# Two-step graph network with nucleus attention: the second step's first tile gathered during the rank stage, and the first step's references copied before the last self additions

## The chip, the cores and the metric

The kernel runs on one core of a Trainium2 chip. TensorE (PE) does the matrix products, VectorE (DVE) the sorting, masking and searching, ScalarE (ACT) the exponentials, GpSimd (POOL) small sums and the indirect transfers, and SyncE (SP) issues the large transfers. The metric is the device time of one launch in microseconds, lower is better. Before the change it is 1792.87 us, the median of three runs (1787.85 to 1796.46).

## The reference

N is 4096 nodes, D is 128 features, the attention projections have 64 columns. R is the adjacency matrix plus the identity, divided by its row sums. Cut to what matters:

```
def _top_p_attention(X, W1, W2, W3):
    q = X @ W1.T @ W2.T
    k = X @ W3.T
    probs = softmax(q @ k.T)
    idx = argsort(-probs); sp = probs sorted; cs = cumsum(sp)
    keep_sorted = cs - sp < 0.9          # the smallest set that holds 0.9
    A = probs * mask
    return A / max(A.sum(-1), 1e-12)

R = S + eye(N); R = R / R.sum(-1)
Z = 0; Xf = X; Xa = X
for n in range(2):
    A = _top_p_attention(Xa, W1, W2, W3)
    Xf = R @ Xf
    Xa = A @ Xa
    Z = Z + Xf @ U1[n].T + Xa @ U2[n].T
h = X + Z
... layer norm of h with gain and shift, then a layer norm of x + that
```

## The kernel before, in words

Both steps of the network run the same three stages. The 4096 rows are cut in 8 blocks of 512, each block in 4 tiles of 128 rows.

**Rank stage** (`rank_block`). For each block PE forms the logits of 512 rows against all 4096 columns, DVE takes the 8 largest of each chunk (MAX8) and sorts out the largest 24 (step 1) or 64 (step 2) of each row (`sort_step`), ACT sums the exponentials. From these DVE computes where the nucleus ends (`stats_step`). This is done for a block while the next one is under way; for the last block it stands by itself at the end of the stage, after 16 sort steps for its last tile. A row whose nucleus doesn't fit the sorted numbers is called hard. Its number goes into `list_dram`, block by block: POOL issues 4 indirect transfers for each block once DVE has placed its rows. Beside it PE multiplies with the adjacency matrix (`adj_part`), whose 64 parts of 1 MB SP loads into a ring of 4 buffers (`adj_in`); each load waits until PE has used the buffer's last content. Before a part that holds the diagonal is used, POOL adds the identity to it (`add_self`).

**Tiles of hard rows.** When all of the list is written, POOL fetches 128 of its entries (`gid`, `gids`), then by indirect transfers the rows' features, references (`href`, `hrefs`) and largest exponentials (`htop`, `htops`). PE transposes the tile, forms its q and its 16 logit products, ACT exponentiates, and DVE searches each row's threshold (`halve`, `chord`, then two passes, MAX8 and sorting). Where a row isn't settled by the sorted 40 numbers, a branch of 24 more sums over the whole row is run (`tile_settle`, `dve.If`). The resulting cuts and norms go to `cut_dram` and `norm_dram` by two indirect transfers.

- In step 1 there is one tile. In program order POOL does: 4 fetches of `gather(0)`, `add_self` of block 6, `add_self` of block 7, then in the loop the copies `gid_out`, `htop_out`, `href_out`, and then `gather(1)`. The next tile's fetch is always made, even where there is none. DVE's search reads the copies. DVE takes the low half of the next tile's q (L1676, `prepare(c + 1)`) at the end of its search. PE and ACT meanwhile finish the adjacency product of blocks 6 and 7.
- In step 2 there are four. The first is gathered, transposed, exponentiated and searched by itself between the rank stage and the loop over the blocks, the others are searched within that loop. Ahead of the first tile stand the last block's z terms (`z_terms` on PE, `other_copy` on ACT, `add_x` on POOL, `z_rows` on DVE), each in two halves.

**Mix stage.** For each block PE forms the transposed logits with the cuts subtracted, ACT exponentiates, DVE masks, PE weighs. In step 1 the adjacency's rows are summed beside it; in step 2 the layer norms are.

The order of the work is written out by hand on each engine. An engine goes through its instructions in order, and a wait holds up all that stands behind it. SP's loads are one queue: in step 1 (L434 to L437) `flow_load` runs through all 64 parts, with the stores of the cuts (`rank_store`) between them, and in step 2 (L441) the stores of block i - 2 come after the 8 loads of block i.

Of the kernel before, what the change touches and what calls it, by code (L numbers as in the profile page):

```python
# [6 lines left out]
FP32 = mybir.dt.float32  # L7
# [8 lines left out]
def gnn_kernel(  # L16
# [71 lines left out]
    LIST = N + (PAIRS - 1) * P  # L88
    LAG1 = 3
# [5 lines left out]
    with ctx:  # L95
# [189 lines left out]
        def step_sems(s):  # L285
# [10 lines left out]
            if s == 0:  # L296
                names += ["h_l", "h_exp", "h_done", "m_l_ps", "m_exp_done"]
                names += ["r_n_ps", "r_n_sb", "m_n_ps", "m_y_sb", "m_yt_ps", "m_yt_sb", "xa_out"]
                names += ["sum_act", "sum_dve", "xf_scaled"]
            else:  # L300
                names += ["slot_full", "slot_read", "h_read"]
                names += ["r_z_ps", "r_zo_sb", "r_zx_sb", "r_z_sb", "m_z_ps", "m_z_add", "var_sb", "rstd_sb", "centred", "normed", "res_sb"]
# [88 lines left out]
        def _(sp):  # L391
# [8 lines left out]
            for s in range(STEPS):  # L400
                g = S[s]

                def rank_loads(i, first):

                    for r in range(PARTS):
                        if not (first and r < RING):
# [5 lines left out]

                def rank_store(i):

                    sp.wait_ge(g["st_cut"], i + 1)
                    rows = bass.ds(i * TB, TB)
                    with nc.allow_non_contiguous_dma(reason="cuts go out in row order"):
                        sp.dma_start(cut_dram[s][bass.ds(i * BI, BI), :].rearrange("(t p) o -> p (t o)", p=P),
                                     ncut[:, rows]).then_inc(g["cut_out"], 16)
                        if s > 0:  # L420
                            sp.dma_start(ref_dram.rearrange("(p t) o -> p (t o)", p=P)[:, rows],
                                         ncut[:, rows]).then_inc(g["cut_out"], 16)
                        for dst, src in ((norm_dram, norm), (top_dram, top_exp)):
                            sp.dma_start(dst[s].rearrange("(p t) o -> p (t o)", p=P)[:, rows],
                                         src[:, rows]).then_inc(g["cut_out"], 16)
# [7 lines left out]
                if s == 0:  # L433
                    for n in range(NB * PARTS):  # L434
                        flow_load(n)
                        if n >= 12 and n % FLOWS == 0 and (n - 12) // FLOWS < NB:
                            rank_store((n - 12) // FLOWS)  # L437
                else:
                    rank_loads(0, True)
                    rank_loads(1, False)  # L440
                    with sp.Fori(2, NB) as i:  # L441
                        rank_loads(i, False)
                        rank_store(i - 2)
# [72 lines left out]
        def _(pool):  # L516
# [32 lines left out]
            for s in range(STEPS):  # L549
# [21 lines left out]
                assert JQ == TB and PARTS == NB  # L571
                SELF_BEFORE = {0: (0, 1), 1: (2,), 2: (3,), 4: (4,), 5: (5,)}
                if s > 0:
                    add_self(0)
                for i in range(NB):
                    if s == 0:
                        for a in SELF_BEFORE.get(i, ()):
                            add_self(a)
                    else:
                        if i < RING - 1:  # L580
                            add_self(i + 1)
                        add_x(i, 0)
                        if RING - 1 <= i < NB - 1:
                            add_self(i + 1)
                        add_x(i, 1)
                    pool.wait_ge(g["st_place"], i + 1)
                    for t in range(i * TB, (i + 1) * TB):
# [4 lines left out]
                            bounds_check=N - 1, oob_is_err=False).then_inc(g["listed"], 16)  # L592
                pool.wait_ge(g["listed"], 16 * T)
                if s > 0:
                    pool.wait_ge(S[s - 1]["xa_out"], 16 * NB)
                pool.wait_ge(g["counted"], 1)

                if s == 0:
# [15 lines left out]
                    gather(0)  # L614
                    for a in range(FLOWS, NB):
                        add_self(a)
                    with pool.Fori(0, tiles) as c:
                        pool.wait_ge(g["h_x"], c * 48 + 48)
# [4 lines left out]
                        pool.wait_ge(g["h_ref"], c + 1)  # L623
# [14 lines left out]
                        pool.wait_ge(g["h_out"], c * 32 + 32)  # L638
                    pool.sem_inc(g["h_done"], 1)
                else:  # L640
                    sweeps = pool.value_load(count[0:1, 0:1], min_val=1, max_val=SWEEPS)

                    def gather_tile(r, c):

                        st = tile_slot(c)
                        if c >= 2:
                            pool.wait_ge(g["h_out"], r * (PT * 32) + (c if c == PT + 1 else c - 1) * 32)
                        pool.dma_start(gids[:, st, :], list_dram[s][bass.ds(r * (PT * P) + c * P, P), :]).then_inc(g["h_gid"], 16)
                        pool.wait_ge(g["h_gid"], r * (PT * 16) + (c + 1) * 16)
                        pool.sem_inc(met, 1)  # L650
                        nc.gpsimd.indirect_dma_start(
                            out=xgs[:, st, :], out_offset=None, in_=source,
                            in_offset=bass.IndirectOffsetOnAxis(ap=gids[:, st, 0:1], axis=0),
                            bounds_check=N - 1, oob_is_err=False).then_inc(g["h_x"], 16)
                        pool.wait_ge(g["cut_out"], 64 * NB)
                        for dst, src in ((hrefs, ref_dram), (htops, top_dram[s])):
                            nc.gpsimd.indirect_dma_start(
                                out=dst[:, st:st + 1], out_offset=None, in_=src,
                                in_offset=bass.IndirectOffsetOnAxis(ap=gids[:, st, 1:2], axis=0),
                                bounds_check=N - 1, oob_is_err=False).then_inc(g["h_ref"], 16)  # L660
# [43 lines left out]
                    gather_tile(0, 0)  # L704
# [18 lines left out]
        def _(pe):  # L723
# [5 lines left out]
            for s in range(STEPS):  # L729
# [122 lines left out]

                def ranks(i):
# [10 lines left out]
                if s == 0:  # L864
                    pe.wait_ge(g["r_o_sb"], FLOWS)
                    for j in range(0, JT // 4):
                        adj_part(FLOWS, j)
                ranks(NB - 1)
                pe.wait_ge(g["st_tally"], NB)
                if s == 0:  # L870
                    to_rows(FLOWS - 1)
                    for j in range(JT // 4, FLOWS * JQ):
                        adj_part(FLOWS, j)
# [7 lines left out]
                if s == 0:  # L881
# [25 lines left out]
                    for j in range(FLOWS * JQ, JT):  # L907
# [71 lines left out]
                else:  # L979
                    sweeps = pe.value_load(count[0:1, 0:1], min_val=1, max_val=SWEEPS)  # L980

                    def tile_rows(r, c):

                        pe.wait_ge(g["h_x"], r * (PT * 16) + (c + 1) * 16)
                        nc.tensor.transpose(psT[:, 0, :], xgs[:, tile_slot(c), :], ident[:]).then_inc(g["h_xt"], 1)

                    def tile_q(r, c):

                        pe.wait_ge(g["h_xts"], r * PT + c + 1)
                        nc.tensor.matmul(psQ[:, 0:P], wq[:], xgT[:], start=True, stop=True).then_inc(g["h_q"], 1)  # L990

                    def tile_logits(r, c, n, bank):

                        if n == 0:
                            pe.wait_ge(g["h_qlo"], r * PT + c + 1)
# [1219 lines left out]
```

## Time and profile before

| | us |
|---|---|
| median of three runs | 1792.87 |
| the profiled execution | 1791.29 |
| its span, first to last instruction | 1789.7 |
| PE busy in the span | 1536.5 (86%) |
| DVE busy | 1335.8 (75%) |
| ACT busy | 785.9 (44%) |
| POOL busy | 231.0 (13%) |

The mean granted clock of PE is 0.934 of full speed. The page also cuts the span in 40 slices of 44.7 us and gives the busy share of each engine in tenths; in the first step the rank stage lasts to about 337 us, the mix stage starts at about 466; in the second they are about 1227 and 1321. In the timeline a row is: start, duration, engine, line, operation, output<-input, number of instructions, and in brackets the idle time of the engine before it and what ended it. "issue" there is a wait whose releaser the profile doesn't show.

### The profile page before, as it was taken

The page shows a single profiled execution, that of the slowest core. Times are in us where ns is not written, and L with a number is a line of the kernel's source. Part 1 is how long each engine was busy: PE and PEld are TensorE (multiplying, and loading weights), DVE is VectorE, ACT ScalarE, POOL GpSimd, SP SyncE. Part 2 cuts the span into 40 slices and gives each one's busy share as a digit, 9 for nine tenths or more (in the row PEclk, how much of TensorE's full clock was granted, in tenths as well). Part 3 has the DMA queues.
Part 4 walks back from the last instruction along what each step waited for, and adds up shares of the span by engine and source line. Part 5 has one row for each costly group of instructions (what it writes and reads, how often), then busy time and mean ns, then how long its engine had stood idle before and what let it go on. Part 6 is the DMA issues. An engine that isn't in the chain of part 4 may idle for free. (4 is left out here: it accounts for less than half of the span.)

```text
span 1789.7 us, 18143 instructions
## 1 busy us (share of the span) xinstructions
PE 1536.5 (86%) x4753; PEld 885.9 (50%) x4753; DVE 1335.8 (75%) x3740; ACT 785.9 (44%) x1245; POOL 231.0 (13%) x264
## 2 busy tenths in 40 slices
PE   6999999772799999998999999992247878888995
PEld 3556555331455555554555656562124535544553
DVE  4788888408477777776899999994868888897553
ACT  3555555210455555555444444441223424434443
POOL 1010211113000000000011111112010121211322
PEclk9999999976799999999999999995668999999997
DMA  7457665740255555555556666630000000000000
GB/s 241 171 142 147 193 202 165 179 169 6 95 188 193 193 193 193 193 194 206 202 172 185 184 175 185 186 118 2 2 2 1 1 7 6 4 4 7 7 7 12
DMA packets 52364, 211.88 MB, mean 118 GB/s; under 512 B 21760, under 2 KB 30528, under 8 KB 31664
## 3 DMA queue, kind: packets, MB, share of 16 engines
q1 hardware_dynamic: 49008, 210.56, 37.1%
q0 software_dynamic: 3264, 0.30, 0.2%
q8 instruction: 33, 0.54, 0.1%
q14 instruction: 59, 0.48, 0.1%
HBM read 206.63 MB, written 4.45 MB: 118 GB/s over the span
## 5 line engine op out<-in xcount | busy, mean ns | idle before, releaser
L1607 DVE MAX8 cand<-psL 128x8 f32<-128x256 f32 (+1 forms) x640 | 371.1, 581 | 58.9 <-PE psL L818 51.9
L1175 ACT ACTIVATE psL<-psL,umax 128x1024 f32<-128x1024 f32 x256 | 278.5, 1088 | 295.0 <-DVE umax L1601 294.6
L817 PE MATMUL psL<-kA,mq 128*128 128x512 f32 x512 | 299.6, 585 | 7.7 <-DVE mq L1434 7.7
L788 PE MATMUL psO<-adj_in,xn 128*128 128x512 f32 x512 | 242.5, 595 | 3.6 <-DMA adj_in<-in_adjT 1.8
L964 PE MATMUL psO<-ebuf,xn 128*128 128x512 f32 x512 | 241.4, 593 | 0.0
L788 PE MATMUL psO<-adj_in,xf 128*128 128x512 f32 x512 | 240.9, 595 | 0.0
L1868 DVE SCALAR_TENSOR_TENSOR ebuf<-ebuf 128x1024 f32<-128x1024 f32 x128 | 156.7, 1224 | 99.7 <-PE psO L964 93.2
L1313 ACT ACTIVATE ebuf<-psL 128x1024 f32<-128x1024 f32 x128 | 129.8, 1021 | 191.3 <-PE psL L1022 134.7
L818 PE MATMUL psL<-kB,mq 66*128 66x512 f32 x512 | 203.4, 397 | 0.0
L1250 ACT ACTIVATE ebuf<-psL 128x1024 f32<-128x1024 f32 x128 | 131.0, 1023 | 133.8 <-PE psL L936 133.8
L1034 PE MATMUL psO<-xf,xa 128*128 128x512 f32 x340 | 167.6, 616 | 19.0 <-DVE xf L2075 19.0
L1021 PE MATMUL psL<-mq,kA 128*128 128x512 f32 x256 | 151.2, 591 | 10.9 <-DVEq L2068 10.9
L935 PE MATMUL psL<-mq,kA 128*128 (+1 forms) x256 | 148.2, 579 | 3.2 <-DVEq L1835 3.2
L2075 DVE SCALAR_TENSOR_TENSOR xf<-ebuf 128x1024 f32<-128x1024 f32 x85 | 105.9, 1250 | 48.5 <-PE psO L1034 30.2
L817 PEld LDWEIGHTS psL<-kA,mq 128*128 128x128 f32 x512 | 97.3, 190 | 79.0 <-issue 53.9
L788 PEld LDWEIGHTS psO<-adj_in,xn 128*128 128x128 f32 x512 | 95.7, 190 | 77.7 <-issue 64.4
L964 PEld LDWEIGHTS psO<-ebuf,xn 128*128 128x128 f32 x512 | 96.7, 190 | 74.9 <-issue 63.9
L788 PEld LDWEIGHTS psO<-adj_in,xf 128*128 128x128 f32 x512 | 95.8, 190 | 74.6 <-issue 66.0
L818 PEld LDWEIGHTS psL<-kB,mq 66*128 66x128 f32 x512 | 97.7, 191 | 69.6 <-issue 57.8
L561 POOL TENSOR_TENSOR adj_in<-adj_in,ident 128x128 f32<-128x128 f32 x64 | 28.0, 467 | 696.3 <-DMA adj_in<-in_adjT 696.3
L1921 DVE SCALAR_TENSOR_TENSOR xf<-adj_in,htry 128x2048 f32<-128x2048 f32 x48 | 112.6, 2346 | 0.4
L1022 PE MATMUL psL<-mq,kB 66*128 66x512 f32 x256 | 104.4, 408 | 0.0
(353 smaller groups left out, 2050.9 us busy)
## 6 DMA issues: line engine op xcount, KB each, us to landing
adj_in<-in_adjT SPq DMA_DIRECT2D x128, 1024.0 KB, 5.5
adj_in<-in_adj SPq DMA_DIRECT2D x32, 2048.0 KB, 7.6
xaT<-in_xT SPq DMA_DIRECT2D x1, 2048.0 KB, 7.8
xa_dram<-xa SPq DMA_DIRECT2D x8, 256.0 KB, 7.8
out<-t SPq DMA_DIRECT2D x8, 256.0 KB, 2.3
list_dram<-ids,place POOLq DMA_INDIRECT x64, 4.4
rel_prob<-cut_dram SPq DMA_DIRECT2D x32, 2.0 KB
cut_dram<-ncut SPq DMA_DIRECT2D x16, 2.0 KB
```

Source lines behind the costliest of these rows:

```text
L788: last = nc.tensor.matmul(psO[:], fs[:, j, :], adj_in[:, r % RING, j % JQ, :], start=(j == 0), stop=(j == JT - 1))
L817: nc.tensor.matmul(o, qA[:, t * P:(t + 1) * P], kA[:, c:c + BI], start=True, stop=False)
L818: last = nc.tensor.matmul(o, qB[0:DA + 2, t * P:(t + 1) * P], kB[0:DA + 2, c:c + BI], start=False, stop=True)
L935: nc.tensor.matmul(o, kA[:, j * P:(j + 1) * P], mqA(i), start=True, stop=False)
L964: last = nc.tensor.matmul(psO[:], xs[:, j, :], ekept[:, u % 2, hb * BI:(hb + 1) * BI], start=(j == 0), stop=(j == JT - 1))
L1021: nc.tensor.matmul(o, kA[:, j * P:(j + 1) * P], mqA(i), start=True, stop=False)
L1034: last = nc.tensor.matmul(psO[:], xs[:, j, :], kept_unit(n)[:, hb * BI:(hb + 1) * BI], start=(j == 0), stop=(j == JT - 1))
L1175: nc.scalar.activation(ps[:], ps[:], ACT.Exp, bias=umax[:, bass.ds(i * UB + k, 1)], scale=1.0, accum_out=usum[:, bass.ds(i * UB + k, 1)]). ...
L1250: nc.scalar.activation(eraw[:, u % 2, :], psL[buffer(u, MU)][:], ACT.Exp).then_inc(g["m_exp_done"], 1)
L1313: nc.scalar.activation(raw_unit(n), psL[w % 3][:], ACT.Exp).then_inc(g["slot_read"], 1)
L1607: last = v.max(cand[:, t % 2, at + c * 8:at + c * 8 + 8], psL[(turn + k) % 3][:, c * WIDE:(c + 1) * WIDE])
L1868: v.scalar_tensor_tensor(out=ekept[:, u % 2, :], in0=eraw[:, u % 2, :], scalar=1.0, in1=eraw[:, u % 2, :], op0=ALU.is_ge, op1=ALU.mult).th ...
```

## The change

It has three parts. First, in step 1 the three copies are made right after `gather(0)`, before the two `add_self`; the loop copies the next tile's at its end. Second, in step 1 SP issues only 52 of the 64 loads, then the last `rank_store`, then waits until the three fetches of `gather(0)` have landed, and only then issues the last 12; PE does 8 parts' worth of products fewer (j from 16 to 24) before that tile and 8 more after it. Third, in step 2 the first tile's list is fetched after six blocks (`EARLY` is 6), its rows in block 7; PE, ACT and DVE do its q, logits and exponentials around the last block's sorting; the last block's z terms come after the logits, with `z_rows` inside the search; and the position in the list is raised to at least 128 after the sixth block. The stores of the cuts of block i - 2 are moved between the first and second load of block i. Those of the last two blocks signal a semaphore of their own (`cut_late`), and the two tables are filled with ones in step 1.

```
@@ step 1, SP
-                    for n in range(NB * PARTS):
+                    held = FLOWS * PARTS + RING
+                    for n in range(held):
                         flow_load(n)
-                        if n >= 12 and n % FLOWS == 0 and (n - 12) // FLOWS < NB:
+                        if n >= 12 and n % FLOWS == 0:
                             rank_store((n - 12) // FLOWS)
+                    rank_store(NB - 1)
+                    sp.wait_ge(g["h_x"], 48)
+                    for n in range(held, NB * PARTS):
+                        flow_load(n)
+                    for dst in (ref_dram, top_dram[1]):
+                        sp.dma_start(dst..., ones[:, 0:T]).then_inc(S[1]["cut_late"], 16)
@@ step 2, SP
+                        if r == 1 and ended is not None:
+                            rank_store(ended)
@@ step 2, POOL (add_self, add_x and list_rows as before, but for the order)
+                    for i in range(NB - 1):
+                        if i < RING - 1:
+                            add_self(i + 1)
+                        add_x(i, 0)
+                        if i == EARLY:
+                            tile_fetch(0, 0)
+                        if i >= RING - 1:
+                            add_self(i + 1)
+                        add_x(i, 1)
+                        list_rows(i)
+                        if i == EARLY - 1:
+                            pool.wait_ge(g["listed"], 16 * EARLY * TB)
+                            tile_list(0, 0)
+                    list_rows(NB - 1)
+                    add_x(NB - 1, 0)
+                    add_x(NB - 1, 1)
@@ step 1, POOL
+                    gather(0)
+                    kept_copies(0)
+                    for a in range(FLOWS, NB):
+                        add_self(a)
+                    with pool.Fori(0, tiles) as c:
...
                         pool.wait_ge(g["h_out"], c * 32 + 32)
+                        kept_copies(c + 1)
                     pool.sem_inc(g["h_done"], 1)
@@ after the rank stage, PE
                 if s == 0:
                     pe.wait_ge(g["r_o_sb"], FLOWS)
-                    for j in range(0, JT // 4):
+                    for j in range(0, RING * JQ // 2):
                         adj_part(FLOWS, j)
+                else:
+                    tile_rows(0, 0)
+                    tile_q(0, 0)
+                    pe.wait_ge(g["r_exp_done"], NB * UB)
+                    for n in range(NU):
+                        if n >= 3:
+                            pe.wait_ge(g["slot_read"], n - 2)
+                        tile_logits(0, 0, n, n % 3)
                 ranks(NB - 1)
@@ step 2, DVE
+                    if s > 0 and n == SORTS - 4:
+                        tile_q_lo(0, 0)
                     sort_step(TB - 1, n)
...
                     tile_begin(0, 0, NU)
                     for n in range(19):
                         search_step(0, 0, n)
-                        if n == 3:
+                        if n == 2:
+                            z_rows(NB - 1, 0)
+                        if n == 5:
+                            z_rows(NB - 1, 1)
+                        if n == 12:
                             tile_q_lo(0, 1)
```

On POOL, from the first fetch of step 1's tile on, the order before is this (`gid` is the list's entries, `xg` the features, L561 the identity's addition for two blocks, L617 the loop's start):

```order
L603 DMA gid<-list_dram0 128x2
L609 DMA xg<-in_x,gid 128x128
L609 DMA href<-cut_dram0,gid 128x1
L609 DMA htop<-top_dram0,gid 128x1
L561 TENSOR_TENSOR adj_in<-adj_in,ident 128x128 x8
L617 UNCONDITIONAL_BRANCH
L617 ISA
L620 COPY gid_out<-gid 128x2
L621 COPY htop_out<-htop 128x1
L622 COPY href_out<-href 128x1
```

and in the changed kernel, same place:

```order
L658 DMA gid<-list_dram0 128x2
L664 DMA xg<-in_x,gid 128x128
L664 DMA href<-cut_dram0,gid 128x1
L664 DMA htop<-top_dram0,gid 128x1
L673 COPY gid_out<-gid 128x2
L674 COPY htop_out<-htop 128x1
L675 COPY href_out<-href 128x1
L573 TENSOR_TENSOR adj_in<-adj_in,ident 128x128 x8
L682 UNCONDITIONAL_BRANCH
```

The three copies have moved ahead of the 8 additions.

On ACT, from the last exponential of the rank stage of step 2 to the second tile, before (L1175 the rank stage's exponentials, L1159 and L1160 those of the last block's statistics, L1137 the z terms' copies, L1281 and L1286 a tile's transpose and q, L1294 its exponentials):

```order
L1175 ACTIVATE psL,usum<-psL,umax 128x1024
L1159 ACTIVATE ue<-ud 128x16
L1160 ACTIVATE rel_prob<-rel_prob 128x256
L1164 ACTIVATE top_exp<-top_rel 128x4
L1165 ACTIVATE ehalf<-half 128x4
L1137 COPY t<-psT 128x256 x2
L1276 TENSOR_LOAD count
L1276 ISA x2
L1281 COPY xgT<-psT 128x128
L1286 CAST hq<-psT 128x128
L1294 ACTIVATE adj_in,hsum<-psL,hrefs 128x1024 x4
```

and in the changed kernel:

```order
L1217 ACTIVATE psL,usum<-psL,umax 128x1024
L1239 COPY xgT<-psT 128x128
L1244 CAST hq<-psT 128x128
L1252 ACTIVATE adj_in,hsum<-psL,hrefs 128x1024 x2
L1201 ACTIVATE ue<-ud 128x16
L1202 ACTIVATE rel_prob<-rel_prob 128x256
L1252 ACTIVATE adj_in,hsum<-psL,hrefs 128x1024 x2
L1206 ACTIVATE top_exp<-top_rel 128x4
L1207 ACTIVATE ehalf<-half 128x4
L1179 COPY t<-psT 128x256 x2
```

The tile's work has moved ahead of the last block's statistics, with two of its four exponentials in front of the pair that DVE's statistics wait for.

On SP, the last loads of step 1, before (L431 a load, L418 and L424 the stores of a block, L458 the read of the norms at the start of the mix stage):

```order
L431 DMA adj_in<-in_adjT 128x2048 x6
L418 DMA cut_dram0<-ncut 128x4x1
L424 DMA norm_dram0<-norm 128x4
L424 DMA top_dram0<-top_exp 128x4
L431 DMA adj_in<-in_adjT 128x2048 x9
```

and in the changed kernel:

```order
L435 DMA adj_in<-in_adjT 128x2048 x3
L410 DMA cut_dram0<-ncut 128x4x1
L416 DMA norm_dram0<-norm 128x4
L416 DMA top_dram0<-top_exp 128x4
L435 DMA adj_in<-in_adjT 128x2048 x12
L448 DMA ref_dram<-ones 128x32
```

Three loads have moved behind the last block's stores, and the wait for the tile stands in front of the 12.

## Rows read from the trace of the kernel before

**Rows 1.** The page's slices: PE's busy tenths, 44.7 us each.
```profile
PE   6999999772799999998999999992247878888995
```

**Rows 2.** Timeline of DVE, the tile of step 1.
```profile
370.17 0.28 DVE L1676 TENSOR_TENSOR mq<-psT,mq 64x128 fp32r<-64x128 f32 x1 [31.17 <-ACT mq L1218]
378.86 0.16 DVE L1756 TENSOR_REDUCE htotal<-hsum 128x1 f32 x1 [8.40 <-ACT xa L1226]
...
406.48 0.15 DVE L1760 TENSOR_SCALAR hupper<-htop_out 128x1 f32<-128x1 f32 x1 [27.21 <-POOL href_out L622]
...
407.44 4.49 DVE L1702 SCALAR_TENSOR_TENSOR ebuf<-xa,htry 128x4096 f32<-128x4096 f32 x1
...
436.24 4.48 DVE L1688 SCALAR_TENSOR_TENSOR ebuf<-xa,htry 128x4096 f32<-128x4096 f32 x1
...
452.47 0.28 DVE L1676 TENSOR_TENSOR mq<-psT,mq 64x128 fp32r<-64x128 f32 x1
```

**Rows 3.** Timeline of POOL, the tile of step 1.
```profile
356.92 0.60 POOL L603 DMA_DIRECT2D gid<-list_dram  x1 [12.88 <-issue]
363.08 1.07 POOL L609 DMA_INDIRECT xg<-in_x,gid  x1 [5.56 <-DMA gid<-list_dram]
...
404.13 1.69 POOL L561 TENSOR_TENSOR adj_in<-adj_in,ident 128x128 f32<-128x128 f32 x4 [35.68 <-DMA adj_in<-in_adjT]
...
406.26 0.18 POOL L622 COPY href_out<-href 128x1 f32<-128x1 f32 x1
...
410.16 2.68 POOL L609 DMA_INDIRECT xg<-in_x,gid  x1 [2.25 <-DMA gid<-list_dram]
...
418.34 4.92 POOL L609 DMA_INDIRECT htop<-top_dram,gid  x1 [0.30 <-issue]
```

**Rows 4.** Timeline of PE, the same stretch.
```profile
332.78 3.70 PE L788 MATMUL psO<-adj_in,xn 128*128 128x512 f32 x8 [1.82 <-DMA adj_in<-in_adjT]
...
368.24 0.45 PE L887 MATMUL psT<-ident,xg 128*128 128x128 f32 x1 [16.71 <-DMA htop<-top_dram,gid]
...
377.13 7.03 PE L788 MATMUL psO<-adj_in,xn 128*128 128x512 f32 x16
...
385.40 27.63 PE L788 MATMUL psO<-adj_in,xn 128*128 128x512 f32 x64
...
424.44 0.48 PE L887 MATMUL psT<-ident,xg 128*128 128x128 f32 x1 [10.01 <-DMA htop<-top_dram,gid]
```

**Rows 5.** Stretch; busy of PE, PEld, DVE, ACT, POOL; clock; DMA share; GB/s.
```profile
330.00:345.00 15.00, 12.86 (x37) 5.97 (x36) 5.38 (x29) 0.89 (x3) 3.89 (x4) 1.00 0.99 390
```

**Rows 6.** Timeline of POOL, the fetch of step 2's first tile.
```profile
1241.80 0.58 POOL L648 DMA_DIRECT2D gids<-list_dram  x1 [2.30 <-issue]
1244.95 1.05 POOL L651 DMA_INDIRECT xgs<-xa_dram,gids  x1 [2.57 <-DMA gids<-list_dram]
```

**Rows 7.** Timeline of DVE, end of step 2's rank stage and first search.
```profile
1214.89 0.29 DVE L1578 MAX8 top<-cand 128x8 f32<-128x128 f32 x1
...
1217.00 0.17 DVE L1472 SCALAR_TENSOR_TENSOR ue<-usum,ue 128x16 f32<-128x16 f32 x1 [0.65 <-ACT rel_prob L1160]
...
1227.36 0.15 DVE L1667 TENSOR_SCALAR count<-s 128x1 int32<-128x1 f32 x1
...
1229.56 0.61 DVE L1524 SCALAR_TENSOR_TENSOR z<-psT,rinv,t 128x128 f32<-128x128 f32 x2 [1.04 <-POOL t L569]
...
1249.62 0.28 DVE L1901 TENSOR_TENSOR hq<-psT,hq 64x128 fp32r<-64x128 f32 x1 [14.46 <-ACT hq L1286]
1257.32 0.16 DVE L1907 TENSOR_REDUCE htotal<-hsum 128x1 f32<-128x4 f32 x1 [7.42 <-ACT adj_in L1294]
...
1307.38 0.16 DVE L2021 TENSOR_TENSOR hkept<-hkept,habove 128x1 f32<-128x1 f32 x1
```

**Rows 8.** Timeline of ACT, the tile's first exponential.
```profile
1252.14 1.11 ACT L1294 ACTIVATE adj_in<-psL,hrefs 128x1024 f32<-128x1024 f32 x1 [2.54 <-PE psL L1000]
```

**Rows 9.** The page's costliest groups: the half-row sums of step 2's searches.
```profile
L1921 DVE SCALAR_TENSOR_TENSOR xf<-adj_in,htry 128x2048 f32<-128x2048 f32 x48 | 112.6, 2346 | 0.4
```

More of the change, by code:

```diff
@@ L401, in _, with rank_store, rank_loads @@
                 g = S[s]
-                def rank_loads(i, first):
+                def rank_store(i):
+                    sp.wait_ge(g["st_cut"], i + 1)
+                    rows = bass.ds(i * TB, TB)
+                    over = g["cut_late"] if s > 0 and i >= EARLY else g["cut_out"]
+                    with nc.allow_non_contiguous_dma(reason="cuts go out in row order"):
+                        sp.dma_start(cut_dram[s][bass.ds(i * BI, BI), :].rearrange("(t p) o -> p (t o)", p=P),
+                                     ncut[:, rows]).then_inc(over, 16)
+                        if s > 0:
+                            sp.dma_start(ref_dram.rearrange("(p t) o -> p (t o)", p=P)[:, rows],
+                                         ncut[:, rows]).then_inc(over, 16)
+                        for dst, src in ((norm_dram, norm), (top_dram, top_exp)):
+                            sp.dma_start(dst[s].rearrange("(p t) o -> p (t o)", p=P)[:, rows],
+                                         src[:, rows]).then_inc(over, 16)
+                def rank_loads(i, first, ended):
                     for r in range(PARTS):
+                        if r == 1 and ended is not None:
+                            rank_store(ended)
                         if not (first and r < RING):
@@ L411, in rank_loads @@
                         sp.dma_start(adj_in[:, r % RING], adjT[i, :, r * JQ:(r + 1) * JQ, :]).then_inc(g["adj_in"][r % RING], 16)
[L413 to L425, printed above, removed]
                 def flow_load(n):
@@ L569, in add_x, with gather_tile @@
                     nc.gpsimd.tensor_tensor(t2[:, 0:ZT, :], t2[:, 0:ZT, :], xn[:, rows, :], ALU.add).then_inc(g["r_zx_sb"], 1)
[L571 to L578, printed above, removed]
-                    else:
[L580 to L585, printed above, removed]
+                def gather_tile(r, c):
+                    if c >= 2:
+                        pool.wait_ge(g["h_out"], r * (PT * 32) + (c if c == PT + 1 else c - 1) * 32)
+                    tile_list(r, c)
+                    tile_fetch(r, c)
@@ L612, in gather, with kept_copies @@
                                 bounds_check=N - 1, oob_is_err=False).then_inc(g["h_x"], 16)
[L614 to L618, printed above, removed]
+                    def kept_copies(n):
+                        pool.wait_ge(g["h_x"], n * 48 + 48)
                         pool.sem_inc(met, 1)
@@ L871, in _ @@
                     to_rows(FLOWS - 1)
-                    for j in range(JT // 4, FLOWS * JQ):
+                    for j in range(RING * JQ // 2, RING * JQ):
                         adj_part(FLOWS, j)
@@ L906, in _ @@
                     prepare_logits(0)
-                    for j in range(FLOWS * JQ, JT):
+                    for j in range(RING * JQ, JT):
                         adj_part(FLOWS, j)
```

161 lines of the change are left out of this document (87 added, 74 removed).

## The prediction

> **What bounds the kernel now.** I read the page's slices first. PE is full nearly throughout and falls to 2 tenths in slice 10 and to 2, 2 and 4 in slices 28 to 30 [rows 1]. These are the two places where a step goes from ranking to mixing, and the change lies in both. So I read the timelines there, engine by engine, and asked who waits for whom.
>
> In step 1 DVE has the tile's sum at 378.86 and goes on at 406.48, 27.21 us later; the releaser is POOL's copy of the references [rows 2]. POOL had long had the data: it stood at block 7's identity, for a load that came at 404.13, and copied after it [rows 3]. Then DVE searches without a break until 452.47, the low half of the next q [rows 2]. PE needs 27.63 us for block 7 beside that wait, until 413.03, and is then waiting itself for the next tile's fetch until 424.44 [rows 4]. The end of this stage is therefore POOL's copy plus DVE's search, 46 us. Before it there is a second wait: POOL issued the last list transfer by 344.04 and could go on only at 356.92, then the list's own fetch took until 363.08 [rows 3]. The same two waits in step 2 are 2.30 us, and 3.15 from 1241.80 to 1244.95 [rows 6]. What differs is the traffic: in 330 to 345 us the queues are 0.99 busy at 390 GB/s [rows 5], and PE itself waits there for a part [rows 4]. So in step 1 the small transfers stand behind 1 MB loads.
>
> In step 2 DVE ends the last block's statistics at 1227.36. The first tile's search begins at 1257.32, and in the 30 us between DVE works little over 2 [rows 7]. POOL does the z terms, then the list, then the tile. The search goes to 1307.5, with DVE alone busy. Only then can the mixing begin.
>
> **Step 1: the held loads.** After load 51 nothing large is queued until the tile has landed. Part 49 landed at 332.78 [rows 4]; at 1 MB in 2.7 us (390 GB/s, rows 5) parts 50 and 51 are in by 338.2, before the last block's list transfers, which end at 344.04. So I take step 2's waits: 344.04 + 2.30 + 3.15 = 349.49 for the first indirect fetch. From there to PE's transpose it was 368.24 - 363.08 = 5.16 [rows 3, 4], so the tile lands at 354.65 and not at 368.24: 13.6 us earlier. The bounds: nothing, if the wait isn't the traffic, and 13.6. I take the upper one, as the rows of step 2 are the same instructions with idle queues. PE loses the cover: 8 parts' products less before the tile (7.03 us per 8 [rows 4]) are done after it, and the first held load must land before PE ends the logits (8.9 us after the tile). Four loads from a standing start take perhaps 2.3 us and then 2.7 each, so the first has some 4 us to spare.
>
> **Step 1: the copies.** They come at 355.3 now, and DVE isn't held. Its sum comes at 378.86 - 13.6 = 365.3, the search goes on about 0.4 later, and 46.0 us on (452.47 - 406.48) it is at L1676, at 411.7. What is late next is that instruction's other input, the next tile's q. PE ends block 7 at 377.13 - 13.6 + 35.9 (to 413.03) + 6.9 (8 parts) = 406.3. POOL adds block 7's identity as before 8.9 us earlier, at 397.4. There DVE is in its last long pass (436.24 to 440.7, moved by 41, is 395.5 to 399.9). POOL's work beside such passes takes long: the indirect fetches of 1.07 and 1.05 [rows 3, 6] took 2.68 and 4.92 there [rows 3]. So I let the additions wait for the end of the pass and take 1.7 from 400: 401.7. From there 3.7 to the indirect fetch (406.44 to 410.16) and 5.2 to PE, at 410.6, and 1.9 to q (368.24 to 370.17 [rows 2, 4]): 412.5. It decides by 0.8 us. The stage is 452.5 - 412.5 = 40.0 shorter. Against it stand the three copies at the loop's end, in front of the signal for the norms, 0.6 us (405.82 to 406.44 [rows 3]). Step 1: **39.4 us**. Below, if the held loads bring nothing, only the 27.2 of the wait go, less 0.6: 26.6, as the next q would be there at about the same time as the search's end (424.44 + 1.9). Above, no wait for q: 40.2.
>
> The two fills with ones lie behind the last load on SP, which then waits anyway.
>
> **Step 2: the tile ahead.** The list is fetched in block 6's time and the rows in block 7's, some 30 us before PE is free for them, and the tile is filled from the same list. The moved stores hold SP's second load of a block by about one unit of the 16 of a block, and that load is needed 5 units later; I count nothing, and some us if that cover is gone. DVE takes q's low half 4 sort steps before the last, at about 1213.8 (the steps, 0.36 each, end with that of 1214.89 [rows 7]). In the trace a first exponential starts 2.5 us after that instruction (1249.62 to 1252.14), and one is 1.11 and its read 0.2 [rows 7, 8]. So the two in front of the statistics' exponentials end at about 1213.8 + 2.5 + 2.6 = 1218.9, or 1.5 earlier with PE at full clock. These statistics ended at 1217.0 for DVE [rows 7], the pair takes 0.5: DVE goes on at 1219.4, 2.4 later, between 1 and 3. The other two lie in DVE's statistics. The statistics then end at 1229.8, one memset follows, and the search's first instruction is at 1230.6 in place of 1257.32: **26.7 us** earlier. Inside the search now are the two `z_rows`, 0.61 each [rows 7]: 1.2. Their sums on POOL stand behind the list's last 4 transfers, which begin at 1228.9 and run partly beside the passes of 2.35 us [rows 9]. By the row with 4.92 each such instruction may wait for the end of one pass: 2 transfers and `add_x` so come to about 1238, and DVE wants them after three passes, at 1240. I take no wait; above it is 3. The second tile's fetch, about 12 us under the same passes, is through by 1260, and its q is wanted after 12 search steps, near 1270; its exponentials need 8 us, DVE's rest 12. It stays covered. Step 2: 26.7 - 1.2 = **25.5 us**, between 22 and 27.
>
> **The sum.** 39.4 + 25.5 = 64.9. The profiled execution is 1791.29, 1.6 below the median of the runs shown. 1791.3 - 64.9 = 1726.4. All that follows either place moves with it, as the mixing starts only from its cuts.
>
> **The Trainium skill** bears on POOL beside DVE. Its page "SBUF — State Buffer", section "SBUF: two separate sides", says that DVE and GpSimd share a port pair as an exclusive lock for a whole instruction, where a DVE operation with two SBUF inputs meets a GpSimd one, and that whoever comes first blocks the other. The trace agrees for POOL (4.92 beside DVE's 4.49 us passes). For DVE no pass here is longer for it: 4.49 and 4.48. By the page DVE would also start late after each POOL instruction; in step 2 that would be some five starts by up to 1 us, and the sum 1731 instead of 1726.
>
> **The rivals.**
> *The loads aren't what held the list* (12 in 100). Against it rows 5 and 6, for it that the 12.88 has no named releaser. Then step 1 gives 26.6: 1791.3 - 26.6 - 25.5 = 1739.
> *POOL loses beside DVE's passes what it gained* (18 in 100). The identity of block 6 waits for the third held load, about 10 us after the tile; DVE's first long pass begins 11.7 after it (406.48 to 407.44 after a sum that comes 10.6 after the tile). If the load is 2 us later, four additions go between passes of 4.49, and PE gets the part 6 to 10 us late; the gathering for the next q goes with it, so step 1 gives 30 to 35. With 2 or 3 us of waiting for `add_x` in step 2 that is 1791.3 - 32.5 - 23 = 1736.
> *Slower: the search's branch is taken* (3 in 100). The first tile now reads references and largest values while the last two blocks are not yet written. If a single row of a tile got a wrong one, `dve.If` runs 24 sums in two halves of 2.35 us with half a us between, 24 x 4.7 + 12 = 125 us: 1726 + 125 = 1851. The point is one flagged row. In before there are 48 such halves in all, 12 for each of four tiles [rows 9], so no row is flagged, and the first tile's rows are from blocks that are stored; if they weren't full, the page's groups would show more than 48.
> *The change doesn't do what it says in step 1* (3 in 100): the search isn't what ends the stage, because the next tile's fetch can't come before block 7's identity and that comes as late as before. Then only step 2's 25.5 remain: 1766.
>
> **How the numbers follow.** The forecast has 62 in 100, its own range 1721 to 1732. The rivals have 12, 18, 3 and 3, and 2 are left for what I don't see. The range of 8 in 10 is 1716 to 1744: down by what PE at full clock would save at either start of mixing and by the spread of the runs shown, up to both likely rivals and the median's 1.6. About 0.5% (9 us) is what a measurement of this kernel can tell from no change. All but the branch lie far beyond it: faster 0.95, within 0.02, slower 0.03.
>
> **What would show it.** In the changed profile: POOL's first list fetch at about 346 and PE's transpose at 355; no wait of DVE for `href_out`; L1676's counterpart at about 412; the mixing of step 1 starting near 427 instead of 466. In step 2 the search's first sum about 1 us after the count instead of 30, and 48 half-row sums. Wrong would be a long wait of PE for POOL's identity in block 6, of DVE for POOL at `z_rows`, or a fetch of the list that still takes 13 us.

## The result, and the profile after

| | before | after |
|---|---|---|
| median (lowest to highest), us | 1791.10 (1787.85 to 1796.46), 4 runs | 1723.93 (1723.05 to 1725.26), 4 runs |
| the profiled execution, us | 1791.29 | 1724.79 |
| its span; mean granted clock of PE | 1789.7; 0.934 | 1723.2; 0.947 |
| mixing begins in step 1, in step 2 (first matmul, us) | 466.29, 1321.08 | 426.47, 1255.83 |

The ratio is 0.9623, interval 0.9596 to 0.9649: 67 us faster, 5 either way. The forecast was 1726.4.

The page of the changed kernel, PE's slices, against [rows 1]:

```profile
PE   6999999977999999998999999994267979888995
```

Slice 10 has 7 instead of 2. The hole at 28 to 30 is 4, 2, 6 instead of 2, 2, 4.

The timeline of POOL in step 1 (start, duration, engine, line, operation, output<-input, count, idle time before and its releaser), against [rows 3]:

```profile
344.21 0.97 POOL L619 DMA_INDIRECT list_dram<-ids,place  x1 [0.30 <-issue]
348.28 0.60 POOL L658 DMA_DIRECT2D gid<-list_dram  x1 [3.10 <-issue]
351.18 1.07 POOL L664 DMA_INDIRECT xg<-in_x,gid  x1 [2.30 <-DMA gid<-list_dram]
...
356.87 0.18 POOL L675 COPY href_out<-href 128x1 f32<-128x1 f32 x1
366.02 1.69 POOL L573 TENSOR_TENSOR adj_in<-adj_in,ident 128x128 f32<-128x128 f32 x4 [8.96 <-DMA adj_in<-in_adjT]
398.52 4.31 POOL L573 TENSOR_TENSOR adj_in<-adj_in,ident 128x128 f32<-128x128 f32 x4 [30.82 <-DMA adj_in<-in_adjT]
```

The list is fetched 3.10 us after its last transfer instead of 12.88, its own fetch takes 2.30 instead of 5.56, and the copies are done before the identity of block 6. PE in the same stretch, against [rows 4]:

```profile
356.33 0.45 PE L956 MATMUL psT<-ident,xg 128*128 128x128 f32 x1 [10.52 <-DMA htop<-top_dram,gid]
...
379.74 27.63 PE L828 MATMUL psO<-adj_in,xn 128*128 128x512 f32 x64
...
410.49 0.33 PE L956 MATMUL psT<-ident,xg 128*128 128x128 f32 x1 [1.72 <-DMA htop<-top_dram,gid]
...
426.47 0.50 PE L1004 MATMUL psL<-mq,kA 128*128 128x512 f32 x1 [3.33 <-DVEq L1895]
```

The next tile's rows are waited for 1.72 us instead of 10.01. DVE, against [rows 2]:

```profile
366.81 0.14 DVE L1820 TENSOR_SCALAR hupper<-htop_out 128x1 f32<-128x1 f32 x1
...
368.00 4.48 DVE L1762 SCALAR_TENSOR_TENSOR ebuf<-xa,htry 128x4096 f32<-128x4096 f32 x1
...
413.02 0.28 DVE L1736 TENSOR_TENSOR mq<-psT,mq 64x128 fp32r<-64x128 f32 x1
```

There is no wait for `href_out`, and none for the next q. In step 2 DVE shows this, against [rows 7]:

```profile
1179.09 0.18 DVE L1521 SCALAR_TENSOR_TENSOR ue<-usum,ue 128x16 f32<-128x16 f32 x1 [3.10 <-ACT rel_prob L1202]
...
1189.46 0.15 DVE L1727 TENSOR_SCALAR count<-s 128x1 int32<-128x1 f32 x1
...
1190.54 0.16 DVE L1962 TENSOR_REDUCE htotal<-hsum 128x1 f32<-128x4 f32 x1 [0.17 <-DVEq L1444]
...
1242.61 0.16 DVE L2076 TENSOR_TENSOR hkept<-hkept,habove 128x1 f32<-128x1 f32 x1
```

The search begins 1.1 us after the count instead of 30. It lasts 52.1 us, 2.0 more than before. The half-row sums are 48 again, against [rows 9] (count, then busy and mean ns, then idle):

```profile
L1976 DVE SCALAR_TENSOR_TENSOR xf<-adj_in,htry 128x2048 f32<-128x2048 f32 x48 | 112.9, 2353 | 0.3
```

The mixing of step 1 begins 39.8 us earlier, that of step 2 65.25, so step 2 gave 25.4. The span is 66.5 shorter; the last 1.3 us lie behind the start of step 2's mixing and aren't explained.

### The profile page after: what moved, and what is told of

The parts are those of the page before. It is cut to its first block and busy times, and to the rows that moved or that the text cites. A ratio compares the mean times of both kernels' runs of the same rounds, so it can differ in the third digit from the quotient of the medians.

```text
span 1723.2 us, 17953 instructions
## 1 busy us (share of the span) xinstructions
PE 1536.2 (89%) x4753; PEld 886.1 (51%) x4753; DVE 1338.1 (78%) x3740; ACT 786.3 (46%) x1245; POOL 232.6 (13%) x267
## 3 DMA queue, kind: packets, MB, share of 16 engines
HBM read 206.63 MB, written 4.48 MB: 123 GB/s over the span
## 5 line engine op out<-in xcount | busy, mean ns | idle before, releaser
L1069 PE MATMUL psL<-mq,kA 128*128 128x512 f32 x256 | 151.2, 591 | 10.4 <-DVEq L2123 10.4
```

Of the source, the lines that this page charges most:

```text
L1069: nc.tensor.matmul(o, kA[:, j * P:(j + 1) * P], mqA(i), start=True, stop=False)
```

## The experiments

Three comparisons were made, each on one chip with the kernel before beside it. That kernel's median was 1797.44, 1800.93 and 1794.89 there. The second and third also had the changed kernel as control: 1733.69 (ratio 0.9627, interval 0.9614 to 0.9641) and 1727.01 (0.9622, 0.9608 to 0.9636). For the two control runs this was expected:

> The changed kernel itself, as control for the others of this call: 0.9623 of before, within 0.0026.

> The changed kernel, control of this call: 0.9623 to 0.9627 of before.

A ratio is good to 2 or 3 us at best, and the difference of two to about 4 (6 in the first comparison, which is set against the ratio of the result above). So I also read from each trace how long it is from the last list transfer of step 1 to the first matmul of the mixing. In the changed kernel that is 344.21 to 426.47, 82.3 us (81.8 and 81.5 in the controls); before it was 343.07 to 466.29, 123.2.

### Is it the hold? Loads not held

```
- held = FLOWS * PARTS + RING ... sp.wait_ge(g["h_x"], 48)
+ for n in range(NB * PARTS): flow_load(n), stores at n = 12, 18, ... 54
- PE: parts 0 to 3 of block 6 ahead of the tile
+ PE: parts 0 to 5
```

A part here is a load of 1 MB, of which PE makes 8 products. The "8 parts' worth" in the description of the change are 8 calls of `adj_part` with 2 products each (the 7.03 us are x16 in the timeline), so they are two of these 1 MB parts.

> The changed kernel, but step 1's 64 loads go out as their slots come free, as before, and PE does block 6's parts as early as before; the copies stay ahead. Theory (the small list transfers stand behind 1 MB loads): POOL's first list fetch comes some 13 us after the last list transfer again instead of 3.1, PE's transpose of the tile at 368 instead of 356.3, the search and the start of mixing some 12 us later: 1724 + 12 = 1736 (1734 to 1739). Rival (the wait has another cause, and the loads were held for nothing): the fetch at 348, 1722 to 1726.

Measured: 1743.58, ratio 0.9698 (0.9679 to 0.9718), 13 us above the changed kernel's ratio, 6 either way. From the last list transfer to the mixing it is 98.1 us, 15.9 more. POOL:

```profile
364.58 0.60 POOL L653 DMA_DIRECT2D gid<-list_dram  x1 [15.28 <-issue]
370.41 1.07 POOL L659 DMA_INDIRECT xg<-in_x,gid  x1 [5.24 <-DMA gid<-list_dram]
...
411.51 9.71 POOL L568 TENSOR_TENSOR adj_in<-adj_in,ident 128x128 f32<-128x128 f32 x4 [33.45 <-DMA adj_in<-in_adjT]
```

Both waits are back, 12.2 and 2.9 longer, and the rival (the fetch at 348, no time lost) is out. Block 7's identity also falls among DVE's long passes and takes 9.71 instead of 1.69 to 4.3. All of this edit, which also puts the stores back behind the loads, is worth the forecast's 13.6, or a little more.

### How much traffic does it take? The hold alone undone on SP

The same, but PE keeps its 4 parts, so only 4 loads can go out.

> The changed kernel, but SP does not wait for the tile before load 52; PE still does only 4 parts of block 6 ahead of the tile. So four more loads of 1 MB go out, one as each of the 4 parts is used, from about 334 to 345, and the rest after the tile. Theory (the queue must be empty, in proportion to what is in it): those four need 11 us, so the queues are busy until about 347 to 350 and the list fetch comes 3 to 6 us later than in the changed kernel: 1727 to 1731. Rival (any load under way costs all of it): 1736. Rival (only the long queue of before costs): 1724.

Measured: 1737.95, ratio 0.967 (0.965 to 0.969), about 8 us more than the changed kernel; 91.9 us to the mixing, 9.7 more. POOL:

```profile
361.56 0.60 POOL L653 DMA_DIRECT2D gid<-list_dram  x1 [12.96 <-issue]
```

With four loads the wait for the list is about what it was with the long queue of the kernel before (12.88); my 3 to 6 us were too few. By the list's wait this is the first rival, that any load under way costs all of it (its time, 8 more and 6 either way, can't tell the two apart). But by the loads alone it is odd: the last of the four goes out at 349.26, one takes 2.7 us by [rows 5], and POOL waits until 361.56. The queues in that stretch (busy of PE, PEld, DVE, ACT, POOL; clock; DMA share; GB/s):

```profile
350.00:355.00 5.00, 0.00 (x0) 0.00 (x0) 0.00 (x0) 0.00 (x0) 0.00 (x0) 0.79 1.09 57
```

They are full with 57 GB/s, where the 1 MB loads moved 390 [rows 5]. Of the 848 packets of these 5 us 814 are under 512 bytes; nearly all of the bytes are in the 34 others, the rest of a load. SP's rows show whose the small ones are. First the changed kernel:

```profile
335.79 0.40 SPq L410 DMA_DIRECT2D cut_dram<-ncut  x1
```

Then this one:

```profile
322.33 23.82 SPq L435 DMA_DIRECT2D adj_in<-in_adjT  x6
346.20 0.43 SPq L410 DMA_DIRECT2D cut_dram<-ncut  x1
```

The last block's three stores (2 KB each, in packets under 512 bytes) stand on SP behind loads that wait for their slot. They go out 10.4 us later, of which 3.4 are the rank stage's. In the changed kernel they stand 8.4 us ahead of the last list transfer, here 1.4, beside the four. So it was in the kernel before, whose list transfers ran from 339.24 to 343.07:

```profile
341.63 0.43 SPq L418 DMA_DIRECT2D cut_dram<-ncut  x1
```

### Loads or stores? Each alone

```
loads not held, stores ahead:      - sp.wait_ge(g["h_x"], 48)
loads held, stores beside the list: + sp.wait_ge(g["st_place"], NB)
                                      rank_store(NB - 1)
```

> The changed kernel, but SP does not wait for the tile before load 52; the last block's three stores stay ahead of that load, as in the changed kernel. So it differs from the run with loads not held (SP only) in the place of the three stores alone. There the list fetch came 13.0 us after the last list transfer, and after the 1 MB loads the queues were busy for 7 us more with packets under 512 bytes at some 40 GB/s. Theory L (1 MB loads under way hold the list): the list fetch is 10 us or more after the last list transfer, 0.967 of before as there. Theory S (the stores' small packets, queued behind the loads and beside the list, hold it): it comes after 3 to 5 us, at most 6, and the time is within 3 us of the changed kernel, 0.962 to 0.964.

> The changed kernel with all its held loads, but SP gives out the last block's three stores only when the last places are known, so that they run beside the four list transfers with no 1 MB load under way. Theory S (the stores' small packets hold the list): the list fetch comes 6 to 10 us after the last list transfer instead of 3.1, the time is 3 to 6 us longer. Theory L: the fetch comes after 3 to 4 us; the references' fetch may wait a little for the stores; within 1.5 us of the changed kernel.

Measured: 1740.39 and 1737.12 against the control's 1733.69, that is 6.7 and 3.4 us more (ratios 0.9657, 0.9642 to 0.9673, and 0.9645, 0.963 to 0.9659; by these 5.4 and 3.2 more, 4 either way, so the second isn't clear of the noise by its time). From the last list transfer to the mixing it is 87.6 and 87.0 us instead of 81.8. POOL, first with the loads not held and the stores ahead:

```profile
352.57 0.97 POOL L618 DMA_INDIRECT list_dram<-ids,place  x1 [0.30 <-issue]
360.67 0.60 POOL L657 DMA_DIRECT2D gid<-list_dram  x1 [7.13 <-issue]
```

Then with the loads held and the stores beside the list, and the queues in that stretch and in the last 6 us of POOL's wait, in the columns of above:

```profile
347.25 0.39 SPq L410 DMA_DIRECT2D cut_dram<-ncut  x1
...
351.85 0.97 POOL L620 DMA_INDIRECT list_dram<-ids,place  x1 [0.30 <-issue]
360.90 0.60 POOL L659 DMA_DIRECT2D gid<-list_dram  x1 [8.08 <-issue]
```

```profile
347.00:361.00 14.00, 6.43 (x15) 2.50 (x14) 0.53 (x4) 0.19 (x1) 3.99 (x5) 0.90 0.04 1
354.00:360.00 6.00, 0.00 (x0) 0.00 (x0) 0.00 (x0) 0.00 (x0) 0.00 (x0) 0.84 0.00 0
```

The control:

```profile
354.69 0.60 POOL L658 DMA_DIRECT2D gid<-list_dram  x1 [2.64 <-issue]
```

Neither theory holds alone. The control waits 2.64 us for the list. Loads alone make it 7.13, stores alone 8.08, both 12.96: 4.5 and 5.4 add up to 9.9, and 10.3 was measured (9.9 against the 3.10 of the first changed profile). The stores do it with the queues 4% busy, and from 354 to 360, while POOL waits, nothing at all moves on them. So it isn't their bytes. Nor is it the program: POOL's fetch of the list waits for the list transfers' semaphore and for the count, and only the fetch of the references behind it waits for the stores'. Why the signal of the list's end comes so late the profile doesn't show.

### Is it the copies?

```
  gather(0)
- kept_copies(0)
  for a in range(FLOWS, NB): add_self(a)
  loop over tiles:
+     kept_copies(c)
```

> The changed kernel, but the three copies stand behind both additions of the identity again, as before; the loads stay held. Theory (DVE's search waits for href_out, and POOL gives it after block 7's identity, whose part now comes at 398 to 402): DVE has the sum at 366.8 and goes on at about 403.5, 36.7 us later; the mixing starts 36 us later: 1724 + 36 = 1760 (1757 to 1763). That would leave to the held loads alone 3 us against the kernel with neither. Rival (terms simply add, 27 for the copies): 1751.

Measured: 1761.51, ratio 0.98 (0.9778 to 0.9822), 32 us more, 6 either way; 116.1 us to the mixing, 33.9 more. The time alone doesn't tell my 36 from the rival's 27, the trace does. DVE:

```profile
402.14 0.15 DVE L1819 TENSOR_SCALAR hupper<-htop_out 128x1 f32<-128x1 f32 x1 [33.95 <-POOL href_out L675]
```

The wait is the price, to a tenth. It is 2.8 less than I expected: with DVE waiting, block 7's identity takes 1.69 and not 4.31. So the parts of the change are no sum. With the copies late the hold is worth 7.4 us (123.5 in the next run less 116.1), with the copies ahead 15.9.

### Step 2 alone

The hold and the copies are both undone, step 2 is as changed.

> Step 1 as before (loads not held, PE's parts as before, copies late), step 2 as changed. Theory (the two places add up): step 1's 39.4 come back: 1724 + 39.4 = 1763 (1761 to 1767), 0.984 to 0.986 of before. Rival (one part's gain needs the other): under 1757 or over 1770.

Measured: 1770.07, ratio 0.9845 (0.9825 to 0.9866), 40 us more, 6 either way; 123.5 us to the mixing, as before (123.2). The two places add up. Within step 2 only the order of two exponentials and the place of the stores were varied (below); what the early fetch, the early logits and the moved `z_rows` give each wasn't measured.

### The two exponentials in front

```
  tile_rows_copy(0, 0); tile_q_hi(0, 0)
- for n in range(2): tile_exp(...)
  stats_prob(NB - 1)
+ for n in range(NU): tile_exp(...)
```

> The changed kernel, but on ACT in step 2 the last block's two exponentials for the probabilities come before all four of the tile's, not after two of them. Theory (DVE waited 3.10 us for rel_prob because of the two in front, 0.65 before the change): that wait falls to about 0.7, DVE ends the statistics and starts the search 2.4 us earlier, the tile's exponentials still end before it; 2.4 us faster than the changed kernel. Rival (the tile's exponentials or the second tile then end late and take it back): under 1 us. Its control runs in the same call.

Measured: 1733.49 against 1733.69; ratio 0.962 (0.9607 to 0.9633) against 0.9627. The mechanism is there:

```profile
1184.45 0.17 DVE L1519 SCALAR_TENSOR_TENSOR ue<-usum,ue 128x16 f32<-128x16 f32 x1 [0.65 <-ACT rel_prob L1202]
```

The wait is 0.65 instead of 3.10. The time tells no difference: 0.2 us between the medians, 1.3 between the ratios, each with an uncertainty above 2. From step 1's first mixing matmul to step 2's it is 827.94 us against 829.15, 1.2 less. That the 2.4 us reach the end isn't shown.

### More of it, and where it turns

```
  step 1, PE: - wait_ge(h_x, n*48 + 48)   + wait_ge(h_row, n*16 + 16)
  (the rows' fetch signals h_row, the other two h_x), and the edit above
```

> The changed kernel with two edits. (1) As in the earlier run, ACT takes the two statistics' exponentials of step 2 before the tile's: 2.45 us less waiting of DVE. (2) In step 1, PE's transpose of the tile's rows waits for the rows' fetch alone and no longer for the references' and the largest values' fetches, which POOL issues 1.37 and 2.68 us after it. The logits then start 2.7 us earlier, the first exponential finds the references there, the sum and DVE's search come 2.5 us earlier; the next tile's q comes 2.7 us earlier too, so it doesn't take the place. Together 5 us less than the control of this call, ratio to before 0.960 against 0.9627. Rival (the references land later than the logits, or the two gains fall where another engine is late): 2.5 us or less.

Measured: 1727.83 against 1727.01 (ratios 0.9628, 0.9612 to 0.9644, and 0.9622): no gain. Step 2 shows its part again: from step 1's first mixing matmul to step 2's it is 826.95 us against 830.19, though the controls themselves differ there by 1.0. Step 1 should have given 2.5 more and lost 0.7, 82.2 us to the mixing against 81.5. What is left of step 2's gain doesn't show in the time: in the profiled execution the rank stage of step 1 is 0.6 longer and what lies behind step 2's first mixing matmul 1.6, where the edits change nothing. Step 1's timelines, POOL, DVE and PE:

```profile
368.57 5.86 POOL L573 TENSOR_TENSOR adj_in<-adj_in,ident 128x128 f32<-128x128 f32 x4 [9.05 <-DMA adj_in<-in_adjT]
```

```profile
368.65 4.64 DVE L1760 SCALAR_TENSOR_TENSOR ebuf<-xa,htry 128x4096 f32<-128x4096 f32 x1
...
416.01 0.28 DVE L1734 TENSOR_TENSOR mq<-psT,mq 64x128 fp32r<-64x128 f32 x1 [1.67 <-ACT mq L1286]
```

```profile
374.58 8.80 PE L828 MATMUL psO<-adj_in,xn 128*128 128x512 f32 x16 [1.89 <-POOL adj_in L573]
```

DVE's first pass now begins 0.08 us after POOL's additions for block 6. These take 5.86 instead of 1.69, PE waits for them, ends block 7 later, and the next q comes after the search's end. The tile's sum had come only 1.4 us earlier after the last list transfer, not 2.5: from PE's transpose to it are 10.9 us instead of 10.2, as PE took 0.63 us, half speed, for more of the logit products. This is the forecast's second rival, set off by an edit meant to help, and smaller than I had it: the way from the sum to the next q is 2.3 us longer, not 4 to 9. In the changed kernel the additions end at 367.71 and the pass begins at 368.00: it was missed by 0.3 us. A version that lets the held loads go when the rows are there, and not the references, might give the additions up to 2.7 us more (the distance of the fetches); it wasn't tried.

### The moved stores of step 2

```
  loop over the 8 parts of a block:
-     if r == 1: rank_store(ended)
      load
+ rank_store(ended)
```

> The changed kernel, but in step 2 the stores of the cuts of block i-2 go out behind all 8 loads of block i again, and not behind the first. Forecast's term: moving them cost nothing. Undoing it: POOL's fetch of the first tile's references waits for block 5's stores about 20 us longer, to the second half of block 7, and behind it on POOL stands the addition of x for the second half of block 6's z. If that addition is needed before (PE's counts wait for it at three quarters of the block), the rank stage ends some us later: 0 to 5 us slower than the control. Rival (the stores behind the first load hold its successor and cost): 1 to 3 us faster than the control.

Measured: 1739.54, ratio 0.9696 (0.9682 to 0.971), 12.5 us more than the control. POOL and PE:

```profile
1163.05 1.00 POOL L609 DMA_INDIRECT hrefs<-ref_dram,gids  x1 [23.24 <-DMA top_dram<-top_exp]
```

```profile
1168.42 0.59 PE L917 MATMUL psT<-hard,before 128*128 128x4 f32 x2 [8.88 <-DVE z L1573]
```

POOL waits for block 5's stores with the addition of x behind it, and PE with its counts for the z that needs it. DVE's count comes at 1202.33 instead of 1191.99. I had the chain right and its price, 0 to 5 us, too low. The forecast counted the moved stores as free on SP's side; what it doesn't say is that the tile ahead rests on them. Whether they would gain anything without it wasn't tried.

### POOL's load beside the search

```
  gather_tile(0, 1)
+ 12 x tensor_tensor(yn[:, 0:2], xn[:, 0:2], xn[:, 2:4], add)
  tile_store(0, 0)
```

> The changed kernel with 12 more additions on POOL (128x256, two SBUF inputs, into a buffer that nothing reads then), right behind the second tile's fetch, beside DVE's search of the first tile in step 2; nothing waits for them until the first tile's cuts are stored. Theory (lock in both directions: an addition of 0.7 us waits for a DVE pass of 2.35 to end, and DVE's next instruction waits for it): the additions show 2 to 3 us each beside the passes, DVE's instructions behind a pass show 0.3 to 0.6 us instead of 0.16 to 0.22, and the search of 52.1 us gets 3 to 8 us longer. Rival (only POOL waits): the search stays at 52.1 within 0.5 and so does the time.

Measured: 1734.35, 7.3 us more than the control (ratio 0.966, 0.9642 to 0.9678). POOL and DVE:

```profile
1222.87 13.40 POOL L747 TENSOR_TENSOR yn<-xn 128x256 f32<-128x256 f32 x12
```

```profile
1223.67 0.76 DVE L2003 SCALAR_TENSOR_TENSOR hparts<-hsums,htarget 128x5 f32<-128x5 f32 x1
...
1225.27 0.75 DVE L2008 SCALAR_TENSOR_TENSOR hend<-hroot,hupper 128x1 f32<-128x1 f32 x1
...
1229.26 2.90 DVE L1978 SCALAR_TENSOR_TENSOR xf<-adj_in,htry 128x2048 f32<-128x2048 f32 x1
```

The control has 0.23, 0.22 and 2.35 there. From the tile's sum to `hkept` it is 57.1 us (1196.82 to 1253.87) instead of 52.1 (1193.08 to 1245.14), inside the 3 to 8 us that I had expected. The other 2.3 us of the time aren't in this search: from mixing to mixing the trace has 5.7 more (835.84 against 830.19). An addition took 1.1 us on average, not 2 to 3, as the first 6.4 of the 13.4 us met only short instructions of DVE. Both sides wait.

## Why the prediction was right, and where it wasn't

- **The held loads, 13.6.** The size held: the list fetch came at 348.28 (forecast 346.3), PE's transpose at 356.33 (354.65); 1.1 us of each difference lies in the rank stage, whose last list transfers came that much later. The cause was half right. I put the whole wait down to the 1 MB loads. About half of it was the last block's stores, which the new order on SP also frees from behind those loads. The first rival was thus half true. That it cost nothing was luck: the change removes both, and I had not reckoned with the stores.
- **The copies and the search.** DVE had the sum at 366.49 (forecast 365.3) and wasn't held. Forecast for the next q was 412.5, decided by PE, with the search at its end at 411.7; it came at 413.02 with no wait, 46.5 us after the sum (366.49). PE's side was as forecast, ACT's half of q was ready at 412.27. The search itself took what I had given it, but from a sum that came 1.2 later. So the search decided, and the order of the two was the wrong way round.
- **Step 1, 39.4.** Measured 39.8 between the starts of mixing. It is so close by two errors that cancel: the rank stage before it was 1.1 longer, and the stage by itself gave 41.0. I had taken off 0.8 for the next q, which wasn't waited for, and 0.6 for the copies at the loop's end, which don't show: from the next q to the mixing it is 13.45 us, before 13.82.
- **Step 2, the delay of 2.4 us.** The wait grew from 0.65 to 3.10, by 2.45. Part of it is PE's clock, as in the row that I took it from: it ran those logits at half speed (below).
- **Step 2, the search.** `z_rows` had no wait, as I had chosen. The search is 2.0 longer and not 1.2. The rest, 0.8, is DVE beside POOL: L1994 showed 0.48 instead of 0.16, L1996 0.63 instead of 0.22, one pass 2.69 instead of 2.35 (POOL has the list's last transfer and the two additions of x there). Here I followed row 2's "4.49 and 4.48" and let DVE lose nothing. The Trainium skill ("SBUF — State Buffer", section "SBUF: two separate sides") has the lock block whoever comes second, a DVE instruction with two SBUF inputs too. The twelve additions agree with it, 5.0 us for DVE. The 1731 that I had worked out from that rule was too high all the same: POOL has so little there that DVE lost 0.8. Two of the rows, from the changed kernel:

```profile
1197.56 0.63 DVE L1996 SCALAR_TENSOR_TENSOR htry<-hroot,hupper 128x1 f32<-128x1 f32 x1
...
1206.83 2.69 DVE L1976 SCALAR_TENSOR_TENSOR xf<-adj_in,htry 128x2048 f32<-128x2048 f32 x1
```

- **Step 2, 25.5.** Measured 25.4, in part by luck. From the last sort step to the search's first sum it is 16.0 us instead of 42.4, which gives 26.4 (forecast 26.7), and the longer search takes 2.0 of it. That would be 24.4; 0.5 more came between step 1's mixing and the last sort step and 0.5 between the search and step 2's mixing, and neither was in the forecast.
- **The rivals.** The collision of block 6's identity with DVE's first pass, the heart of the second one, was one small edit away; there the time from the sum to the next q was 48.6 us (367.38 to 416.01) instead of 46.3 (368.21 to 414.50). The branch wasn't taken: 48 sums.

## What to carry to other kernels

A queue written out in order holds more than what is seen to wait in it: when a load that waits for its buffer moves, ask what stands behind it. Small stores beside a list that is waited for can cost as much as megabytes (5.4 and 4.5 us here), and both belong behind or well ahead of it. A forecast that hits can still hide errors that cancel: check its terms, not only its sum. Before an engine that shares its way with another is sped up, look at which of its instructions will then meet the other's long ones: a tile's sum that came 1.4 us earlier ended in a mixing 0.7 us later here.

## What was not expected of the hardware

- Three stores of 2 KB beside the four list transfers held the list's landing by 5.4 us, with the queues 4% busy at 1 GB/s.
- Of DVE's small instructions many take up to 0.76 us instead of 0.16 to 0.23 beside additions or indirect transfers of POOL (0.48 and 0.63 in the changed kernel, 0.75 and 0.76 beside the twelve additions), and twelve additions of 128x256 next to the passes cost DVE 5.0 us in 13.4.
- PE lost its clock in step 2 though it was never idle for long. It was 8.00 of 8 us busy to 1168, then 0.84 of 3 and 0.19 of 2, and the logits from 1173.65 were granted 0.50, which is the 1.2 GHz level, and the two idle stretches before them were 2.16 and 2.46 us. The stretches of the changed kernel, in the same columns:

```profile
1160.00:1168.00 8.00, 8.00 (x26) 4.57 (x25) 7.67 (x41) 3.60 (x6) 2.38 (x3) 1.00 0.07 2
1168.00:1171.00 3.00, 0.84 (x5) 0.30 (x2) 2.83 (x15) 1.96 (x5) 1.62 (x2) 1.00 0.02 1
1171.00:1173.00 2.00, 0.19 (x2) 0.00 (x0) 1.82 (x9) 0.27 (x1) 0.00 (x0) 0.83 0.00 0
1173.00:1178.00 5.00, 4.35 (x10) 3.51 (x11) 2.62 (x12) 1.76 (x3) 0.00 (x0) 0.50 0.02 3
```
